# Attention scores on one core: three PSUM banks for the query side and three for the key side, where there were four and two

## What is computed

```python
k = (x @ Wk).reshape(B, H, T, hs)      # B 32, H 6, T 1024, hs 16
q = (x @ Wq).reshape(B, H, T, hs)
v = (x @ Wv).reshape(B, H, T, hs)
wei = einsum('bhtd,bhsd->bhts', q, k) * C ** (-0.5)
wei = softmax(where(tril(ones((T, T))), wei, -inf), axis=-1)
out = einsum('bhts,bhsd->bhtd', wei, v).reshape(B, T, C) @ Wp + bp
```

## Time and profile before

| | |
|---|---|
| median of 3 runs | 2945.53 us (2943.88 to 2947.05) |
| the profiled execution, its own time | 2944.34 us |
| its span, first to last instruction | 2942.6 us |
| TensorE busy | 2759.9 us (94%) |
| VectorE busy | 2299.2 us (78%) |
| ScalarE busy | 2020.0 us (69%) |
| GpSimd busy | 1153.5 us (39%) |
| granted TensorE clock, mean | 0.972 |
| VectorE's maxima of the query units (L965) | 2304 of them, 1135.1 us, 549 ns each |
| exponentials (L928) | 1344 + 384, 743.7 + 208.6 us, about 600 ns each |
| first and last reading of a query unit | 1020.1 us, 2417.0 us |

### The profile page before, as it was taken

The page is one execution under the profiler, slowest core; times in us unless marked ns, Lnnn a source line. Parts: engine busy times, 40 slices in busy tenths (PEclk is TensorE's granted clock), DMA queues, the critical chain, the costliest instruction groups (busy, mean ns, idle before and its releaser), DMA issues. The chain is left out here.

```text
span 2942.6 us, 86412 instructions
## 1 busy us (share of the span) xinstructions
PE 2759.9 (94%) x29306; PEld 1686.9 (57%) x29306; DVE 2299.2 (78%) x4591; ACT 2020.0 (69%) x3943; POOL 1153.5 (39%) x1999
## 2 busy tenths in 40 slices
PE   3899999999999499999999999999999996899995
PEld 2555555555555266666666666666666663455553
DVE  3576676676765499999999999999999984678886
ACT  1677777777776267777777777777777773576774
POOL 0153443444434544444444444444444431224444
PEclk9999999999999699999999999999999998899998
DMA  1113233232232466666666666666666644234545
GB/s 34 43 54 113 75 112 107 80 112 89 98 112 91 127 117 118 118 119 118 119 118 116 116 116 117 117 117 117 120 117 118 121 83 109 81 92 139 143 129 151
DMA packets 923408, 316.04 MB, mean 107 GB/s; under 512 B 848785, under 2 KB 906418, under 8 KB 923314
## 3 DMA queue, kind: packets, MB, share of 16 engines
q1 hardware_dynamic: 923314, 314.77, 47.3%
HBM read 113.35 MB, written 99.88 MB: 72 GB/s over the span
## 5 line engine op out<-in xcount | busy, mean ns | idle before, releaser
L965 DVE TENSOR_REDUCE at_unit_max<-at_ps_queries 128x1 f32<-128x512 f32 (+4 forms) x2304 | 1135.1, 549 | 88.5 <-PE at_ps_queries L853 86.2
L928 ACT ACTIVATE at_probs<-at_ps_keys 128x512 f32<-128x512 f32 x1344 | 743.7, 604 | 388.0 <-PE at_ps_keys L868 383.4
L853 PE MATMUL at_ps_queries<-at_turned 96*128 96x128 bf16 (+3 forms) x3456 | 634.3, 274 | 33.0 <-DMA at_turned<-at_spread 32.2
L868 PE MATMUL at_ps_keys<-at_turned 128*128 128x128 bf16 (+3 forms) x3456 | 648.6, 275 | 1.8 <-ACT at_probs L928 1.5
L803 POOL TENSOR_TENSOR at_v<-at_stacks,at_one 128x128 f32<-128x128 f32 x192 | 76.5, 399 | 815.1 <-DMA at_stacks<-qkv_rows 815.0
L888 PE MATMUL at_ps_values<-at_probs,at_v 128*32 128x128 f32 x10752 | 373.3, 276 | 6.4 <-ACT at_probs L928 6.3
L868 PEld LDWEIGHTS at_ps_keys<-at_turned 128*128 128x128 bf16 x3456 | 237.5, 97 | 240.0 <-ACT at_probs L928 88.5
L853 PEld LDWEIGHTS at_ps_queries<-at_turned 96*128 96x128 bf16 x3456 | 289.2, 97 | 124.3 <-DMA at_turned<-at_spread 33.9
L888 PEld LDWEIGHTS at_ps_values<-at_probs,at_v 128*32 128x32 f32 x10752 | 269.6, 109 | 120.4 <-ACT at_diag_probs L928 70.2
L928 ACT ACTIVATE at_diag_probs<-at_ps_keys 128x512 f32<-128x512 f32 x384 | 208.6, 595 | 8.3 <-PE at_ps_keys L868 5.3
L822 POOL TENSOR_SCALAR_AFFINE_SELECT at_diag_probs<-at_diag_probs 128x1024 f32<-128x1024 f32 x192 | 209.5, 1091 | 0.0
(11 more groups left out here) (209 smaller groups left out, 4969.0 us busy)
## 6 DMA issues: line engine op xcount, KB each, us to landing
qkv_rows<-cb_packed SPq DMA_DIRECT2D x32, 1536.0 KB, 8.2
at_stacks<-qkv_rows SPq DMA_DIRECT2D x192, 256.0 KB, 3.3
cb_x<-in_x_dram SPq DMA_DIRECT2D x32, 384.0 KB, 3.7
cb_x_again<-in_x_dram SPq DMA_DIRECT2D x32, 384.0 KB, 4.5
x_after_conv<-cb_x SPq DMA_DIRECT2D x32, 384.0 KB, 5.0
attention_rows<-at_att SPq DMA_DIRECT2D x384, 32.0 KB, 2.2
ff_att_rows<-attention_rows SPq DMA_DIRECT2D x32, 384.0 KB, 4.0
ff_x<-x_after_conv SPq DMA_DIRECT2D x128, 96.0 KB, 2.4
```

The costliest lines, as they stand in the source:

```text
L853: mm = pe.matmul(pq[:, u % QBANKS, c0:c0 + n], QT[0:STACK, slot, qb * P:(qb + 1) * P], KT[0:STACK, slot, k0:k0 + n], start=(c0 == 0), stop ...
L868: mm = pe.matmul(pk[:, bank_k, c0:c0 + n * P], KT[:, slot, kb * P:(kb + 1) * P], QT[:, slot, q0 * P:(q0 + n) * P], start=(c0 == 0), stop=True,
L928: act.activation(probs, pk[:, (slot * NU + k) % KBANKS, :], ACT.Exp, scale=scale).then_inc(S["probs"], 1)
L965: dve.tensor_reduce(peaks, scores, AX.X, ALU.max).then_inc(S["unit_max"], 1)
```

## The change

Two constants. With them the number of banks changes on both sides, and with it which earlier unit each unit waits for; the code that uses them is unchanged.

```diff
     SLOTS = 6
     BATCHES = {4: (0, 1, 2, 3, 4), 8: (5, 6, 7, 8)}
-    QBANKS, KBANKS = 4, 2
+    QBANKS, KBANKS = 3, 3
     QDIAG = [[(qb, qb * P, P) for qb in range(g, g + HALF)] for g in (0, HALF)]
```

## The result

The changed kernel takes 2983.52 us in the median of 4 runs (2982.68 to 2984.15), against 2944.70 us for the kernel before on the same chip: 38.8 us slower, ratio 1.0131 (95% interval 1.0113 to 1.0148). The profiled execution has a span of 2982.4 us, 39.8 us more than before. Forecast were 2981.5 us and +36.

A forecast was written before the change was run, and what follows sets the result against it. TensorE was taken as the bound, VectorE close behind at 92%. Per head +0.315 (query) - 0.125 (key) = +0.19 us, over 192 heads 36 us, gives 2981.5 us; range 2967 to 2995.

The forecast's parts named there:

- The pause before unit 11: TensorE must stand 0.32 us in each head before query unit 11 until VectorE has read unit 8.
- units 9 and 10: Query units whose awaited reads end slightly late, unit 10 some 0.04 us; both delays were to be swallowed by the next.
- The sum: Per attention head +0.315 - 0.125 = +0.19 us, over 192 heads 36 us; the ordinary head 7.44 us.
- the saving on the key side: Key loads' waits for ScalarE's exponentials all vanish with a third key bank: near 0.125 us a head, bounds 0 and 0.15.
- The term for the query bank: Cost of going from four query banks to three, from TensorE waiting on VectorE's reads: +0.315 us a head.
- key 0's 0.10 against 0.055: Key 0 follows the maximum's transpose by 0.10 us instead of 0.055 in three heads a lap; counted as 3 x 0.06.
- Unit 5: This query unit asks for the read of unit 2, over at 1507.73; its product starts at 1507.76, fitting by 0.03 us.
- The transposes' cover: Output transposes, delayed to end at 1511.81, still finish 0.06 us before VectorE's reciprocal; otherwise up to 0.05 us is added.
- Weight loads not hidden: Rival: late weight loads of query units 5, 10 and 11 count in full, 70 us, 3015 us; chance 0.07.
- Paid back before the values: Rival: 0.09 us gaps before each of two values batches absorb the late start, 35 us return, 2947 us; chance 0.06.
- Faster: Rival: three query banks are enough, only the key waits' saving stays, -24 us, 2921 us; chance 0.04.
- The clock: Rival: pauses in every head lower TensorE's clock for one head in ten, 82 us on top, 3063 us; chance 0.02.

The follow-up runs named there:

- kernel 4: The changed kernel with VectorE's read of query unit 8 halved to 256 columns: 2928.67 us, ratio 0.9956 to the kernel before.
- kernel 5: The changed kernel with VectorE's read of query unit 3 halved to 256 columns: 2982.63 us, ratio 1.0138 to the kernel before.
- kernel 1: The kernel before with three query banks instead of four, two key banks kept, one bank unused: 2986.10 us, ratio 1.0152.
- kernel 2: The changed kernel with query unit 11 issued behind key 6 instead of ahead of the output transposes: 2940.69 us, ratio 0.9997 to the kernel before.
- kernel 6: The changed kernel with the output transposes issued ahead of query unit 11: 2946.07 us, ratio 1.0013 to the kernel before.
- kernel 9: The changed kernel, output transposes ahead of query unit 11, 384- and 512-column units at places 5 and 6 exchanged: 2945.11 us, ratio 1.0011 to the kernel before.

## Why the prediction was right, and where its terms were not

**The pause before unit 11** came as worked out: 0.32 us (0.265 at unit 11, 0.06 at units 9 and 10, which I had let the next one swallow whole; it is the same time), release 0.05 us. Kernels 4 and 5 show its cause, and that VectorE's total work is not it.

**The sum**, +0.19 us a head, was measured as +0.199; the ordinary head 7.47 against 7.44, the mean 7.492 against 7.48. That the mean is nearer than the ordinary head is in part luck: two errors have opposite signs. The ordinary head gained 0.03 us from the key side and not 0.06. Around the jump it went the other way: there the kernel before lost 0.69 us a lap against six ordinary heads, and the changed kernel 0.15. The forecast took away the key waits in this (0.38 us) and left TensorE's pause as it was; the pause shrank too, from 0.27 us to 0.06, and unit 5 lost 0.09 us in the fourth head of a lap.

**The step that was mis-sized** is the saving on the key side, 0.125 us a head as a term of its own. All those waits did go, but kernel 1 shows that most went through the pause: the third key bank itself is worth 0.03, and all of that behind the jump. The term for the query bank, taken alone, is 0.23 and not 0.315. I had taken the two waits from the same rows as if one did not move the other. The sum held, since it was made for both together. (One item in the saving is also larger than the rows quoted for it: key 0's 0.10 against 0.055 is 0.045 us, and the sum counts 0.06; what follows it on the queue, 0.013, makes up the difference but was not named.)

**Unit 5**, "it just fits, by 0.03", lost 0.02: as key 1 came earlier, the row shows 0.49 us from unit 4 to the values (1485.93 to 1486.42) against 0.47 before. In the changed kernel this is small; in kernels 2, 6 and 9, which removed the pause, it was part of what I had left out.

**The transposes' cover** held: they end at 1489.85 + 0.38 = 1490.23, and the reciprocal starts at 1490.28.

**The rivals.** Weight loads not hidden: no; unit 11's load begins at 1489.62 and its product at 1489.63. Paid back before the values: no; 0.31 us from key 6 to the values against 0.32. Faster: no; which earlier unit is asked for decides, and VectorE has read unit 8 only at 1489.57. By the Trainium skill (Perfetto Trace Analysis, "Optimization Strategy") the bubbles on the key side spoke for a third bank there; the bubbles went, and larger ones came where the bank was taken. The clock: no; it was 1.00 over the stretch of 174 heads with a pause of a quarter of a microsecond in each head, so the oscillation told of in the Trainium skill (TensorE: Matmul & The Clock Gate, "A second HAM failure mode: psum-queue depth-cycling") does not appear here.

## What to carry to other kernels

When banks move from one side to another, write down for each unit which earlier read it now asks for and when that read ends, and look for the ring that closes over both engines; the sum of waits in the profile shows the side that has too few, but not what the other side can spare. Waits on one queue are not additive: one pause feeds the other engine and hides its wait, so price two halves of a change together, or run each alone. A shortened operation on the ring and one off it are a cheap pair to prove such a ring.

## What the runs showed of the hardware

TensorE's pause at a loop's jump back is not a fixed cost: it differs between kernels whose jump is the same. In the kernel before, the load of key 6 waits there for ScalarE, and the load of the values came at 1526.28, 0.57 us after that of key 6:

```profile
1525.71 0.11 PEld L868 LDWEIGHTS at_ps_keys<-at_turned 128*128 128x128 bf16 x2
1526.28 0.18 PEld L888 LDWEIGHTS at_ps_values<-at_probs,at_v 128*32 128x32 f32 x7 [0.45 <-ACT at_probs L928]
```

In the changed kernel key 6 waits for nothing, and it is 0.45 us:

```profile
1497.43 0.21 PEld L868 LDWEIGHTS at_ps_keys<-at_turned 128*128 128x128 bf16 x2
1497.88 0.19 PEld L888 LDWEIGHTS at_ps_values<-at_probs,at_v 128*32 128x32 f32 x8 [0.24 <-ACT at_probs L928]
```

Against an ordinary head of the same kernel, the values come 0.27 us later at the jump in the kernel before and 0.06 in the changed one; in kernel 1, whose two key banks are as before, it is 0.07.

I read it so: a load that waits holds up the instructions of the jump behind it, and a load that does not lets them run ahead of the products. That reading was not tested by itself, and two kernels do not fit its simple form. In kernel 6 key 6 is last before the jump and waits for nothing, and the values still come 0.16 us late (key 6 at 1486.55, the values at 1487.02). In kernel 2 unit 11 is last and waits for nothing, and they come 0.10 us late. It may be how far ahead of the jump the last waiting load stands that decides: from the start of that load to the load of the values it is 0.57 us in the kernel before (key 6), 0.67 in kernel 6 (unit 11, one unit earlier, held 0.04 us) and 0.79 in the changed kernel (unit 11, with the transposes and key 6 behind it). Kernel 2 stays unexplained, and none of this is shown as a cause.
